# Expert rows split 112 + 64, partial results added by TensorE, the middle stage's front tile by tile, and fewer fills between GpSimd's scatters, in a transformer layer with 64 experts

## The reference, cut to what matters

```python
# the mixture of experts: 64 experts, 6 for each token, 96 places in each expert
scores = softmax(x @ gate_weight.T)
topk_w, topk_i = top_k(scores of the best 3 of 8 groups, 6)
slot = flat * 96 + minimum(pos, 95)                 # pos: how many tokens chose the expert before
buf = zeros((64 * 96, 256)).at[slot].set(x[tok])    # rows go to their experts
out = (silu(buf @ Wg) * (buf @ Wu)) @ Wd            # Wg, Wu: 176 x 256, Wd: 256 x 176
y = sum(out[slot] * topk_w) + shared(x)             # back to the tokens; shared: 352 wide
# the recurrence between the two mixtures
h = a * h + sqrt(1 - a**2) * (i * x)                # a, i: sigmoids of x @ Wa.T, x @ Wx.T
```

## Time and profile before

| | us |
|---|---|
| median of 3 runs | 1286.99 (1285.45 to 1289.58) |
| the profiled execution | 1283.71 |
| its span | 1281.9 |

### The profile page before, as it was taken

How to read it: one execution, slowest core, us unless ns; L and a number is a source line. 1 busy time by engine, 2 the same in 40 slices (tenths; PEclk the granted TensorE clock), 3 DMA queues, 4 the chain that set the end, 5 groups by cost and what they waited for, 6 DMA issues and landing times.

```text
span 1281.9 us, 18696 instructions
## 1 busy us (share of the span) xinstructions
PE 985.2 (77%) x6520; PEld 594.9 (46%) x6520; DVE 523.4 (41%) x1532; ACT 728.9 (57%) x960; POOL 423.7 (33%) x408
## 2 busy tenths in 40 slices
PE   4886868778887788787554999955587863999973
PEld 3633323322332323222334999943344442999962
DVE  7744431156221233230441333337776741333327
ACT  2285989999999999999101444414434400344420
POOL 3100000000222003234043565530098985556550
PEclk9878888998999998999686999976698976999985
DMA  9990000000111001100583999748133434899947
GB/s 352 394 393 31 1 1 1 1 17 1 42 47 37 17 16 60 39 20 6 148 254 92 292 295 289 177 118 273 50 116 117 123 109 106 243 293 284 261 72 305
DMA packets 94927, 176.11 MB, mean 137 GB/s; under 512 B 13119, under 2 KB 46880, under 8 KB 94833
## 3 DMA queue, kind: packets, MB, share of 16 engines
q1 hardware_dynamic: 58416, 130.55, 30.4%
q0 software_dynamic: 23616, 28.44, 10.4%
q10 hardware_dynamic: 12800, 15.93, 4.5%
HBM read 107.30 MB, written 83.72 MB: 149 GB/s over the span
## 4 chain that ended last, share of the span: by engine, by line
PE 32%; DVE 5%; DMA 3%; issue 3%; SPq 2%; POOL 2%; ACT 2%; DVEq 1%; POOLq 0%; ACTq 0%
PE PS L1323 13%; PE PS L1334 8%; PE PS L1261 4%; PE PS L1393 2%; PE PS L1310 2%; POOL expert_in L307 2%; SPq L1116 1%; DMA spare_space<-expert_out 1%; DMA normed<-xp 1%; SPq L1117 1%; PE PS L1246 1%; DMA XE<-expert_in 1%; PE PS L1270 1%; DMA expert_out<-ob,yidx 1%; POOL expert_out L1209 1%
## 5 line engine op out<-in xcount | busy, mean ns | idle before, releaser
L307 POOL DMA_INDIRECT expert_in<-xp,didx x192 | 192.9, 1005 | 621.7 <-ACT PR L684 483.9
L679 ACT ACTIVATE PR<-PS 128x1024 f32<-128x1024 f32 (+3 forms) x320 | 275.4, 935 | 55.7 <-PE PS L578 40.7
L684 ACT ACTIVATE PR<-PR 128x2048 f32<-128x2048 f32 (+3 forms) x160 | 272.4, 1705 | 0.0
L1209 POOL DMA_INDIRECT expert_out<-ob,yidx x128 | 180.6, 1411 | 148.2 <-ACT ob L1502 108.3
L587 PE MATMUL PS<-PR,V 128*32 128x512 f32 (+3 forms) x1280 | 164.8, 590 | 80.4 <-ACT PR L684 80.3
L575 PE MATMUL PS<-QT,KT 96*128 96x512 bf16 (+3 forms) x640 | 177.5, 372 | 19.8 <-ACT PR L679 16.9
L1740 DVE SCALAR_TENSOR_TENSOR gta<-gth,PS 88x192 f32<-88x192 f32 x128 | 44.8, 350 | 193.6 <-ACT gth L1492 193.6
L575 PEld LDWEIGHTS PS<-QT,KT 96*128 96x128 bf16 x640 | 59.3, 103 | 130.3 <-ACT PR L679 89.7
L1492 ACT ACTIVATE gth<-PS 88x192 f32<-88x192 f32 x128 | 41.7, 326 | 107.8 <-PE PS L1323 107.8
L1323 PEld LDWEIGHTS PS<-XT,spare_space 128*88 128x88 f32 x960 | 92.5, 164 | 8.8 <-issue 2.6
L1502 ACT ACTIVATE ob<-PS,wslot 96x256 f32<-96x256 f32 x128 | 60.1, 469 | 61.9 <-PE PS L1334 59.6
(11 more groups left out here) (257 smaller groups left out, 1355.3 us busy)
## 6 DMA issues: line engine op xcount, KB each, us to landing
spare_space<-in_wgu SPq DMA_DIRECT2D x60, 352.0 KB
expert_out<-zero SPq DMA_DIRECT2D x2, 8256.0 KB, 50.4
expert_in<-zero SPq DMA_DIRECT2D x2, 7776.0 KB, 39.3
XE<-expert_in ACTq DMA_DIRECT2D x32, 486.0 KB, 9.8
WGU<-in_wgu SPq DMA_DIRECT2D x44, 352.0 KB
spare_space<-expert_out SPq DMA_DIRECT2D x24, 512.0 KB, 6.1
spare_space<-in_wd SPq DMA_DIRECT2D x60, 176.0 KB
shared_space<-in_wgu SPq DMA_DIRECT2D x24, 352.0 KB
```

Of the source, the lines that this page charges most:

```text
L307: pool.indirect_dma_start(out=buf_d[f], out_offset=bass.IndirectOffsetOnAxis(ap=didx[b][:, r, j:j + 1], axis=0), in_=xp[b][:, r, :], in_of ...
L679: act.activation(PR[:, n % 3, 2 * pr:2 * pr + 2, cols(c, s):CW], PS[:, S0 + 2 * pr:S0 + 2 * pr + 2, cols(c, s):CW], ACT.Tanh, scale=1.0 / ...
L684: act.activation(PR[:, n % 3, :, lo:CW], PR[:, n % 3, :, lo:CW], ACT.Exp, scale=SOFT_CAP).then_inc(exp_done, 1)
L1209: pool.indirect_dma_start(out=y_d[f], out_offset=bass.IndirectOffsetOnAxis(ap=yidx[:, n % 4, j:j + 1], axis=0), in_=ob[:, i % EU, :], in_o ...
```

## The change

**Rows 112 + 64.** The gate and up rows of an expert are split in 112 and 64 instead of 88 and 88. The 112 gate rows and the 112 up rows have a column group of their own, and the 64 gate rows and the 64 up rows share one of 128 columns, so gate-and-up are 3 groups x 2 = 6 matmuls. VectorE's second operation becomes two, of 112 x 96 and of 64 x 96. The down weights are loaded in two DMAs, of 112 and of 64 rows.

**Sums on TensorE.** `overflow_rows` becomes `sum_rows`: for each tile the overflow matmul and, when that tile's partial results are loaded, four matmuls with the identity that add them up in PSUM. VectorE's `add_results` is one addition from PSUM, for chunk 0 one of each tile just ahead of its statistics. A tile of the chunk after is loaded as soon as its place is read.

**Tile by tile.** Scaling, turning and copying of a chunk signal each tile of 128 rows; the two PSUM banks alternate by tile, and turning tile 2 waits for the copy of tile 0. The routing scores wait for each tile.

**Order.** In the round c = 1, VectorE makes the statistics for chunk 4's rows alone and then those of chunk 2, and its `slots` and `destinations` stand ahead of `recur_inputs`. On TensorE `place(k)` stands ahead of the sum of chunk c + 2.

**Fills.** GpSimd fills the unused tile only behind every second scatter (`j % 2`).

**The last chunk** is combined and stored in two halves.

```diff
-MH = M // 2
+MA = 112
+MB = M - MA
@@ dispatch_rows
-                    if pause is not None:
-                        n = CT * TOPK * (k - NC) + r * TOPK + j
+                    if pause is not None and j % 2:
+                        n = (CT * TOPK * (k - NC) + r * TOPK + j) // 2
                         if n:
                             pool.wait_ge(paused, n)
                         pool.memset(pause[:], 0.0).then_inc(paused, 1)
@@ weights
                 sp.dma_start(wgu, wgu_d[e]).then_inc(loaded, 16)
-                sp.dma_start(wd, wd_d[e]).then_inc(loaded, 16)
+                sp.dma_start(wd[:, 0, :], wd_d[e, 0:MA, :]).then_inc(loaded, 16)
+                sp.dma_start(wd[0:MB, 1, :], wd_d[e, MA:M, :]).then_inc(loaded, 16)
@@ results
-                if f == 0 and c:
-                    sp.wait_ge(results_free, c)
                 for r in range(CT):
                     i = CT * c + r
+                    if f == 0 and c:
+                        sp.wait_ge(result_psum, i - CT + 1)
@@ turn_rows (turn_recur alike)
+                for r in range(CT):
+                    if r < CT - 1:
+                        pe.wait_ge(row_tile, (CT - 1) * n + r + 1)
+                    else:
+                        pe.wait_ge(rows_ready, k + 1)
+                    if r >= 2:
+                        pe.wait_ge(rowsT_ready, CT * n + r - 1)
+                    for h in range(CH):
+                        at = (r // 2) * C + h * P
+                        last = pe.transpose(PS[:, T0 + r % 2, at:at + P], xp[k % NXP][:, r, h * P:(h + 1) * P], const("ident"))
+                    last.then_inc(rowsT_psum, 1)
@@ gate_up
-                    for j in range(4):
+                    for j, at, width in ((0, 0, MA), (2, MA, MA), (1, 2 * MA, 2 * MB)):
                         for hh in range(CH):
-                            last = pe.matmul(PS[0:MH, 4 + e % 2, j * CAP:(j + 1) * CAP], wgu[:, hh, MH * j:MH * (j + 1)],
+                            last = pe.matmul(PS[0:width, 4 + e % 2, j * CAP:(j + 1) * CAP], wgu[:, hh, at:at + width],
@@ down
-                    for m in range(2):
-                        last = pe.matmul(PS[0:CAP, 6 + e % 2, 0:C], ha[:, e % 2, m, :], wd[:, m, :],
+                    for m, width in enumerate((MA, MB)):
+                        last = pe.matmul(PS[0:CAP, 6 + e % 2, 0:C], ha[0:width, e % 2, m, :], wd[0:width, m, :],
@@ overflow_rows becomes sum_rows
                 for r in range(CT):
-                    last = pe.matmul(PS[:, S0 + r // 2, (r % 2) * C:(r % 2 + 1) * C], WovT[:, (CT * c + r) * P:(CT * c + r + 1) * P], O95[:],
-                                     start=True, stop=True, skip_group_check=True)
-                last.then_inc(ov_psum, 1)
+                    acc = PS[:, S0 + r // 2, (r % 2) * C:(r % 2 + 1) * C] if c else PS[:, (S0, S0 + 1, A0, A0 + 1)[r], 0:C]
+                    pe.matmul(acc, WovT[:, (CT * c + r) * P:(CT * c + r + 1) * P], O95[:], start=True, stop=False, skip_group_check=True)
+                    pe.wait_ge(y_ld[r], 16 * (c + 1))
+                    for j in range(NACC):
+                        last = pe.matmul(acc, const("ident"), GB[:, r, j * C:(j + 1) * C], start=False, stop=(j == NACC - 1), skip_group_check=True)
+                    last.then_inc(result_psum, 1)
@@ TensorE's list
-                if c + 2 < NC:
-                    overflow_rows(c + 2)
                 if c:
                     place(k)
+                if c + 2 < NC:
+                    sum_rows(c + 2)
@@ ScalarE: turned_rows (turned_recur alike; scale_rows and scale_recur signal each tile)
-                act.activation(xnT[:], PS[:, T0:T0 + 2, :], ACT.Copy).then_inc(rowsT_ready, 1)
+                for r in range(CT):
+                    act.wait_ge(rowsT_psum, CT * n + r + 1)
+                    act.activation(xnT[:, :, r * P:(r + 1) * P],
+                                   PS[:, T0 + r % 2, (r // 2) * C:(r // 2 + 1) * C].rearrange("p (h n) -> p h n", h=CH), ACT.Copy)\
+                       .then_inc(rowsT_ready, 1)
@@ VectorE: experts
-                    dve.scalar_tensor_tensor(ha[:, e % 2, :, :].rearrange("p m s -> p (m s)"), bank[:, 2 * CAP:4 * CAP], 0.5,
-                                             gta[:], ALU.mult, ALU.mult).then_inc(act_ready, 1)
+                    dve.scalar_tensor_tensor(ha[:, e % 2, 0, :], bank[0:MA, 2 * CAP:3 * CAP], 0.5, gta[:, 0:CAP], ALU.mult, ALU.mult)
+                    dve.scalar_tensor_tensor(ha[0:MB, e % 2, 1, :], bank[MB:2 * MB, CAP:2 * CAP], 0.5, gta[0:MB, CAP:2 * CAP],
+                                             ALU.mult, ALU.mult).then_inc(act_ready, 1)
@@ VectorE: combine_late
-                for r in range(CT):
+                for lo, hi in ((0, CT),) if c < NC - 1 else ((0, 2), (2, CT)):
+                    for r in range(lo, hi):
@@ VectorE: statistics
+                        if (before, after) == (0, None):
+                            dve.wait_ge(result_psum, r + 1)
+                            added = dve.tensor_tensor(X[:, r, :], X[:, r, :], PS[:, (S0, S0 + 1, A0, A0 + 1)[r], 0:C], ALU.add)
@@ VectorE: add_results
-                for r in range(CT):
-                    dve.wait_ge(y_ld[r], 16 * (c + 1))
-                    tables = GB[:, r, :].rearrange("p (j q n) -> p j q n", j=NACC // 2, q=2)
-                    dve.tensor_tensor(tables[:, :, 0, :], tables[:, :, 0, :], tables[:, :, 1, :], ALU.add)
-                dve.drain()
-                dve.tensor_tensor(GB[:, :, 0:C], GB[:, :, 0:C], GB[:, :, 2 * C:3 * C], ALU.add)
-                dve.drain()
-                xc = X[:, CT * c:CT * (c + 1), :]
-                dve.tensor_tensor(xc, xc, GB[:, :, 0:C], ALU.add).then_inc(results_free, 1)
+                dve.wait_ge(result_psum, CT * (c + 1))
@@ VectorE's list in the middle stage
-                if c:
+                if c == 1:
+                    statistics(None, 0)
+                    statistics(2, None)
+                elif c:
                     statistics(c + 1 if c + 1 < NC else None, c - 1)
...
+                if c == 1:
+                    slots(k)
+                    destinations(k)
                 if c < NC:
                     recur_inputs(c)
                 if c + 2 < NC:
-                    add_overflow(c + 2)
-                if c:
+                    add_results(c + 2)
+                if c >= 2:
                     slots(k)
                     destinations(k)
```

More of the change, by code:

```diff
@@ L1048, in hybrid_kernel @@
         WD_space = keep("WD_space", [P, EU * 2 * C])
-        WD = WD_space[0:MH, :].rearrange("p (e m c) -> p e m c", e=EU, m=2)
+        WD = WD_space[0:MA, :].rearrange("p (e m c) -> p e m c", e=EU, m=2)
         XE = keep("XE", [CAP, 2, EH, RW])
         XT = keep("XT", [P, 2, EH, CH, CAP])
-        gth = keep("gth", [MH, 2, 2 * CAP])
-        gta = keep("gta", [MH, 2 * CAP])
-        ha = keep("ha", [MH, 2, 2, CAP])
+        gth = keep("gth", [MA, 2, 2 * CAP])
+        gta = keep("gta", [MA, 2 * CAP])
+        ha = keep("ha", [MA, 2, 2, CAP])
         ob = keep("ob", [CAP, EU, C])
@@ L1077, in expert_weights @@
             loads = f * len(range(x, E, RING)) + e // RING + 1
-            return wgu, wd, ring_ld[x], 32 * loads
+            return wgu, wd, ring_ld[x], 48 * loads
         def last_user(x):
@@ L1178, in _ @@
                 results(1, c)
-            for c in range(NC):
+            for c in range(NC - 1):
                 sp.wait_ge(combined, c + 1)
                 sp.dma_start(x_rows[:, CT * c:CT * (c + 1), :], X[:, CT * c:CT * (c + 1), :]).then_inc(out_stored, 16)
-            sp.wait_ge(out_stored, 16 * NC)
+            for half in range(2):
+                i = CT * (NC - 1) + 2 * half
+                sp.wait_ge(combined, NC + half)
+                sp.dma_start(x_rows[:, i:i + 2, :], X[:, i:i + 2, :]).then_inc(out_stored, 16)
+            sp.wait_ge(out_stored, 16 * (NC + 1))
         @block.gpsimd
@@ L1375, in turn_recur @@
                     pe.wait_ge(xt_ready, NH)
-                for h in range(CH):
-                    for r in range(CT):
-                        last = pe.transpose(PS[:, T0 + h, r * P:(r + 1) * P], xr[:, r, h * P:(h + 1) * P], const("ident"))
-                last.then_inc(xrT_psum, 1)
+                for r in range(CT):
+                    if r < CT - 1:
+                        pe.wait_ge(recur_tile, (CT - 1) * c + r + 1)
+                    else:
+                        pe.wait_ge(xr_ready, c + 1)
+                    if r >= 2:
+                        pe.wait_ge(xrT_ready, CT * c + r - 1)
+                    for h in range(CH):
+                        at = (r // 2) * C + h * P
+                        last = pe.transpose(PS[:, T0 + r % 2, at:at + P], xr[:, r, h * P:(h + 1) * P], const("ident"))
+                    last.then_inc(xrT_psum, 1)
             def gates(c):
-                pe.wait_ge(xrT_ready, c + 1)
+                pe.wait_ge(xrT_ready, CT * (c + 1))
                 if c:
@@ L1555, in turned_recur @@
```

(21 more changed lines are left out.)

88 lines of the change are left out of this document (32 added, 56 removed).

## The result

In the first comparison the changed kernel takes 1326.18 us (median of four runs, 1320.84 to 1327.72), the kernel before 1286.22 (1281.80 to 1289.58): ratio 1.0305, 95% interval 1.0271 to 1.034. Compared again on another chip it takes 1313.26 (1309.44 to 1316.17), ratio 1.0193 (1.0155 to 1.0232). Both are slower, and both lie outside the forecast range of 1250 to 1286. Each ratio in this text is to runs of the kernel before that were made beside it, on the same chip.

A forecast was written before the change was run, and what follows sets the result against it. TensorE bounds both expert stages, about 150 us each; GpSimd narrowly sets the middle stage's end. Rows -13.5 and middle stage -3.6 sum to -17 us, from a median of 1287.0 to 1270 us; range 1250 to 1286.

The forecast's parts named there:

- Gate and up: Expert stages: 12 records instead of 16, 1.21 us instead of 1.32, a gain of 14.1 us over 128 experts.
- B: Rival, expert stages: weight loads don't bind, gate and up gain 42 us, about 1246 us; chance 0.12.
- D: Rival, expert stages: wide loads take 0.113 us or more whatever the width, 1289 us, no change; chance 0.09.
- The down matmuls keep 256 columns: nothing.: Expert stages: the down matmuls keep their column count, so the row split costs them nothing.
- E: Rival, expert stages: TensorE waits for the next expert's weights, slower, about 1304 us; chance 0.07.
- VectorE's extra operation and the loads: Expert stages: hidden behind TensorE, bare only behind each stage's last expert, 0.6 us; the split down loads hidden too.
- Fills: GpSimd's scatters, middle stage: 36 fills fewer save 10.6 us, at most 7.6 as chunk 7 waits for destinations.
- The middle stage's front: Sums on TensorE, 8.6 us a chunk: later destinations for chunks 5 to 7 cut the fills' 7.6 us to 3.6.
- Two slips: Working: 24 scatter steps a chunk; chunk 4's gates 1.9 us late from 4.7 lost, 1.4 and 1.6 regained.
- Tail: Last chunk in halves: operations +0.5 us, shorter last store -0.6 us, together nothing.
- The sum: Whole kernel: -13.5 for the rows and -3.6 for the middle stage, -17 us, 1270 us; chance 0.50.
- theory S: From the experiments: matmuls over 64 rows use another shape of TensorE than 88 to 128; each change empties it.

The follow-up runs named there:

- e2: Changed kernel with the second down matmul over 96 rows instead of 64, 32 of them zero: 1277.45 us, ratio 0.9908.
- e4: Kernel before with the 112 + 64 split alone, its second down matmul over 96 rows, 32 of them zero: 1277.26 us, ratio 0.9912.
- f2: The kernel of e2 measured again, beside f3: 1270.76 us, ratio 0.9869.
- e1: Kernel before with the 112 + 64 row split and nothing else: 1318.25 us, ratio 1.0234.
- e3: Changed kernel with the row split taken back to 88 + 88 and two loads an expert: 1283.36 us, ratio 0.9985.
- f3: Changed kernel with the second down matmul and the overflow matmul of each sum over 96 rows instead of 64: 1268.72 us, ratio 0.9842.
- f4: Kernel before with the 112 + 64 split over 96 padded rows and the halved fills: 1266.42 us, ratio 0.9821.
- e6: The kernel of f3 in an earlier series, whose profile has stops: 1284.95 us.
- g3: Changed kernel with the 64-row matmul ahead of the 112-row one in each down product: 1313.54 us, ratio 1.0218.
- e7: Changed kernel, weight loads before the second expert stage waiting for the last chunk's destinations: 1332.77 us, ratio 1.0363; its series also holds e4, e6 and another kernel.

## Why the prediction was wrong, step by step

- **Gate and up.** Forecast 1.21 us, cycle 2.08 and loads of 112 columns near 178 ns; measured, once the down matmul is widened (e2), 1.22 in the chain, 2.09 and 177 ns. The pace between the two known widths was right, and rivals B and D fall. The gain is there: 6 to 7 us a stage in e2, e4 and f2, 13 in all.
- **"The down matmuls keep 256 columns: nothing."** This step failed. The columns and the count were looked at and the contraction wasn't: it went from 88 + 88 rows to 112 + 64. Put at nothing, it costs 0.34 x 128 = 44 us and turns the -13 of the rows into +31 (e1: +30.3 measured). No rival held it: E forecast a slower kernel by the stream of weights, and no matmul waits for a load in that stage of the changed kernel.
- **It could be seen.** In the kernel before, only the overflow matmuls contract over 64 rows or fewer. Ahead of them the weight loads of the kernel before stand idle for 0.76 us where the loads of the matmuls ahead, all over 128 rows, stand 0.24 apart, and I read only the matmuls of that group:

```profile
881.63 0.19 PEld L1393 LDWEIGHTS PS<-spare_space,wab 128*128 128x128 f32 x1 [0.24 <-issue]
882.57 1.59 PEld L1354 LDWEIGHTS PS<-O,WovT 64*128 64x128 f32 x8 [0.76 <-issue]
```

  The eight loads over 64 rows have no gap among themselves. In e3 the gap at this place, ahead of the first overflow matmul behind the gates, is 0.76 again; in f3, where that matmul contracts over 96 rows, it is 0.24, like those between the gates' own loads. So the rest of the 0.76 comes of the 64 rows:

```profile
880.70 0.19 PEld L1370 LDWEIGHTS PS<-O,WovT 96*128 96x128 f32 x1 [0.24 <-issue]
```

  The Trainium skill has the rule, in TensorEngine Tiling (Array Packing), Tiling Modes, Key Properties: a change of tiling mode drains TensorE; further on in that page of the Trainium skill, under Performance Considerations, a contraction of up to 64 rows is listed under row tiling. The traces agree: 0.36 us idle ahead of the loads at both changes of an expert in the changed kernel, no such gap between 72, 96, 112 and 128 rows. That page of the Trainium skill gives no price. In the forecast I weighed what it says on weight loads, by which rows don't matter for one load's duration, and not this.
- **VectorE's extra operation and the loads** were hidden, as forecast: the cycles of e2 and f2 leave no room for either.
- **Fills.** Forecast 7.6 us at most, with GpSimd waiting ahead of chunks 5 and 6; measured 5.4 by the ratio, 6 to 8 by the stage, with both waits (1.74 us and 4.49) and steps of 1.28 and 1.57 us in turn. Right.
- **The middle stage's front.** Forecast: chunk sums of 8.6 us, destinations of chunk 4 early by 0.9, -3.6 us with the fills. In the changed kernel a sum takes 10.2, for the same reason as above, and the term was short by 4 x 0.4 = 1.6 us a chunk. Ahead of the first recurrence VectorE waits 8.25 us, not 4 (e3; 6.7 in f3):

```profile
894.94 1.22 DVE L1820 TENSOR_TENSOR X<-X,PS 128x1024 f32<-128x1024 f32 x1 [8.25 <-PE PS L1370]
```

  Chunk 4's destinations come 86.0 us behind the last down matmul in e3 instead of 82.0, and the stage is as long as before (240.8 and 241.2). With the sums widened (f3) they come at 81.4, those of chunks 5 to 7 are some 3 us later than before (2.5 forecast), and the stage takes 236.8, 3 to 4 us less than before: the forecast's numbers. But the fills alone give 233.3, so by these profiles the front itself costs 3 to 4 us; the forecast had charged it 4. The times point the same way without deciding it: f4, which has no tile-by-tile front, is 2 us below f3, with overlapping intervals.
- **Tail:** 38.7 to 39.5 for 39.1 to 39.6. Nothing, as forecast.
- **Two slips** in the working had no weight. From the first to the last scatter of a chunk are 23 steps and not 24, but the usual step is 1.28 us all the same. And 4.7 - 1.4 - 1.6 is 1.7 us late at the end of chunk 4's gates, not 1.9.
- **The sum** of 1270 us is about what the change gives once its short contractions are widened and no stops come: 1277.45 (e2) and 1270.76 (f2) with the down matmul, 1268.72 (f3) with both; with stops it is 1284.95 (e6).

## What to carry to other kernels

When a split changes sizes, price the contraction rows as well as the columns: look in the trace for the idle time of the weight loads at the borders between groups of unlike shapes, not inside them. A matmul over 64 rows between taller ones was cheaper here with eight rows of zeros behind it (1313.26 us and 1272.53); shorter ones were not tried. And before a loss is put down to the change, see whether another launch of the same kernel shows it: here 13 of 40 us were gone on another chip.

## What the runs showed of the hardware

- In the changed kernel the weight loads stand 0.36 us idle at each change between 64 contraction rows and 112 or more (0.33 us in the sums of the middle stage). With the 64-row matmul first (g3) the gap of 0.36 us stands at the change out of 64 rows, and the change into them makes the step 0.18 us longer. No gap of that size stands between 72, 96, 112 and 128 rows, nor among eight loads over 64 rows. Net it was 0.17 us a change in a full stream of float32 matmuls. That TensorE is emptied there is what theory S says; the traces show the idle time and its price.
- Twelve float32 records with 96 moving columns, eight with 112 columns of weights (loads of 177 ns) and four with 128 (192 ns), take 1.22 us in the chain of e2, 0.10 each.
- VectorE and ScalarE stop for 1 to 15 us at places where the program gives them nothing to wait for, in the first profile of the changed kernel and in all four of e7's series, and in none of the other 13 profiles, three of which are of the same code. The cause is open.
